# Three reorderings in a four-layer attention kernel: late next queries, an early first norm, a copy between maxima

## The chip, the cores and the metric

The kernel runs as one launch on one core of a Trainium2 chip. The metric is the device time of that launch in microseconds (us), as the median of several runs; lower is better. One further execution was recorded by the hardware profiler. Engines are PE (TensorE, the matrix unit), DVE (VectorE), ACT (ScalarE), POOL (GpSimd) and SP (SyncE, which here only starts transfers).

## What is computed

Four layers over a float32 input of 4 batches x 512 positions x 256 features, with a context of 4 x 64 x 192:

```
x = L0(x, ctx)   # cross attention (16 heads of 16), norm, feed-forward, residual
x = L1(x, ctx)   # norm, self attention (16 heads of 64); norm, cross attention; norm, gated feed-forward
x = L2(x, ctx)   # four state-space blocks over ctx followed by x
x = L3(x, ctx)   # norm, self attention (16 heads of 16); norm, cross attention; norm, feed-forward
```

The norms and one attention, cut to what matters here:

```
h = (x - mean(x)) * rsqrt(var(x) + eps) * g + b          # over the 256 features
p = exp(s - max(s)) / sum(exp(s - max(s)))               # s = q k^T, one row per query
out = p @ v ;  x = x + out @ Wo + bo
```

## The kernel before

Everything is float32 and feature-major: 128 features lie on the partitions, the 512 positions of a batch in the free dimension, so a linear layer is a row of 128x512 matmuls into one bank of PSUM each. The kernel is three blocks with a barrier between them: the first phase (layers one and two, that is L0 and L1, buffers `a_`), the middle one (the state-space layer, `m_`), which the change leaves alone, and the last phase (L3, buffers `c_`). There is no scheduler: each engine's program is written out by hand, in the order in which it runs, and every engine works strictly through its own list. A step waits with `wait_ge` for the semaphore count of the step it needs. A kernel is built twice, so that counts of steps written later are known. What sets the order around the change is therefore the source itself, separately for `pe`, `act` and `dve`.

In layers one, two and four the batches overlap in turns. A turn `(b, a)` holds the second half of batch `b` and the first half of batch `a = b + 1`; in layer one, small products for batch `n = a + 1` (its queries `query0`, lines 991 to 993, its context keys and values `context`, `keys2`, `values2`) lie between them. `x_of(b)` are two buffers: batch `n`'s rows can only be fetched after batch `b`'s were stored, once `l0 down 1 out` is done on DVE (the SP program, lines 914 to 920). `query0(n)` on PE waits for that fetch; its two results are copied by DVE (line 1259).

`Dense` holds the helpers. A norm is `pe_mean` (line 350), `dve_centre` (384), `act_squares` (368), `pe_var` (360), `act_rstd` (374 and 377), `dve_scale` (392 and 397). `pe_linear` (334) runs one product per output tile, `dve_residual` (405) adds it to x. These share a ring of two PSUM banks, `lin`: each `take` hands out the other bank, together with the step that empties its last contents, for which PE waits:

```
k = self.slots[self.i % len(self.slots)]
self.i += 1
freed, self.prog.emptied[k] = self.prog.emptied.get(k), (steps.sem, steps.at(emptied))
```

In layer two, a turn starts when the self attention of batch `b` ends: its output product `o1` (two tiles of 16 matmuls in the trace, each empties through `dve_residual`), then the first norm of `a` (`n1`) and the second of `b` (`n2`), interleaved step by step; then the queries `q1` of `a` and `q2` of `b`, eight tiles each.

In the last phase `pe_quads`, `act_quads`, `dve_quads` and `pool_self` (lines 663 to 795) run self attention in 16 steps of four units; a unit is one head and 128 queries, its scores fill one bank. In step `i` PE makes the four scores (678, ring `five` of five banks), then the transposes of units 4i-4 to 4i-1 (687, four each, ring `trn` of two banks), and in every second step a product with the values (702). DVE takes the four maxima (722), reciprocals of the sums (730) and copies the transposes of units 4i-3 and 4i-1 out of PSUM (737); ACT does the exponentials (783) and the copies of 4i-4 and 4i-2 (769); POOL divides (794). Unit 4i-1's transposes go into the bank that 4i-3's had, so they wait for DVE's copy of 4i-3.

## Time and profile before

| | us |
|---|---|
| median of 3 runs | 4527.23 (4520.4, 4527.23, 4527.54) |
| the profiled execution, its own time | 4522.28 |
| its span (first to last record) | 4520.2 |
| first phase, to the barrier | about 1440 |
| middle phase | about 2220 |
| last phase | about 850 |

The page gives PE 3775.1 us of busy time (84% of the span), DVE 3056.4, ACT 2351.8 and POOL 2115.0. The share of an engine is an average over three phases of different kind: in the first and the last PE is busy in most slices and the others are not, in the middle one DVE is busy throughout. So the trace has to be read stage by stage, by what PE waits for in each. The three runs lie 7 us apart.

### The profile page before, as it was taken

How to read it: one execution, taken by the hardware profiler on the slowest of the kernel's cores; microseconds unless marked ns; L12 is line 12 of the kernel's file. 1: busy time of each engine (PE TensorE's matmuls, PEld its weight loads, DVE VectorE, ACT ScalarE, POOL GpSimd, SP SyncE). 2: the span in 40 equal slices, each digit the busy share in tenths (PEclk: the TensorE clock that was granted, in tenths of full speed). 3: DMA queues.
4: the chain of work that ended last, by engine and by line, in shares of the span. 5: the costliest groups of instructions: out<-in, count | busy, mean ns of one | idle time of the engine just before them, and what ended most of it. 6: DMA issues, size and time to landing. Idle time of an engine off the chain costs nothing. (4 is left out here: it accounts for less than half of the span.)

```text
span 4520.2 us, 51563 instructions
## 1 busy us (share of the span) xinstructions
PE 3775.1 (84%) x16536; PEld 1949.7 (43%) x16536; DVE 3056.4 (68%) x4176; ACT 2351.8 (52%) x4473; POOL 2115.0 (47%) x2144
## 2 busy tenths in 40 slices
PE   8889999999986688877888788887888767878777
PEld 4434444444442244444444444444444434434343
DVE  4335435373451499998999989999899956464553
ACT  3234323242331477776777667776777634445352
POOL 1002112030120477877787777787777833222130
PEclk9999999999998799999999999999999989899999
DMA  3010000000001433222332233333332110000000
GB/s 144 28 49 17 1 19 1 10 10 10 5 1 44 103 92 85 73 84 78 89 85 80 74 96 88 85 93 84 94 85 73 49 60 1 11 1 12 1 6 5
DMA packets 135962, 228.48 MB, mean 51 GB/s; under 512 B 19280, under 2 KB 118864, under 8 KB 126864
## 3 DMA queue, kind: packets, MB, share of 16 engines
q1 hardware_dynamic: 135696, 225.20, 16.9%
q8 instruction: 135, 2.21, 0.2%
q14 instruction: 131, 1.07, 0.1%
HBM read 192.55 MB, written 32.60 MB: 50 GB/s over the span
## 5 line engine op out<-in xcount | busy, mean ns | idle before, releaser
L2039 POOL TENSOR_TENSOR m_db<-m_u,m_bb 128x512 f32<-128x512 f32 (+1 forms) x1280 | 1465.0, 1163 | 458.3 <-DVE m_hh L1991 455.4
L1991 DVE TENSOR_TENSOR_SCAN m_hh<-psum,m_kept,m_db 128x512 f32<-128x512 f32 (+1 forms) x1024 | 1195.9, 1202 | 29.9 <-POOL m_u L2084 17.5
L1790 ACT ACTIVATE psum<-m_dt,m_am 128x512 f32<-128x512 f32 (+1 forms) x1280 | 818.2, 644 | 407.0 <-DVE m_hh L1991 403.4
L1718 PE MATMUL psum<-cst,m_hh 128*128 128x128 f32 x4608 | 666.7, 286 | 323.5 <-DVE m_yt L2005 207.5
L1718 PEld LDWEIGHTS psum<-cst,m_hh 128*128 128x128 f32 x4608 | 525.6, 145 | 761.8 <-DVE m_yt L2005 424.0
L1728 PE MATMUL psum<-m_ys,cst 128*128 128x512 f32 x1024 | 553.0, 623 | 0.0
L2005 DVE SCALAR_TENSOR_TENSOR m_yt<-psum,m_bc,m_yt 128x512 f32<-128x512 f32 x600 | 437.6, 729 | 54.7 <-PE psum L1718 53.7
L794 POOL TENSOR_SCALAR a_pr<-a_pr,a_ri 128x512 f32<-128x512 f32 x256 | 173.8, 692 | 602.9 <-DVE a_ri L611 602.9
L794 POOL TENSOR_SCALAR c_pr<-c_pr,c_ri 128x512 f32<-128x512 f32 x256 | 173.7, 692 | 406.7 <-DVE c_ri L730 402.4
L1802 ACT ACTIVATE m_ys<-psum,m_bc 128x512 f32<-128x512 f32 x512 | 343.9, 672 | 24.1 <-PE psum L1718 22.7
L651 ACT ACTIVATE a_pr<-psum,a_mx 128x512 f32<-128x512 f32 x256 | 173.4, 682 | 264.4 <-DVE a_mx L601 264.4
L1604 PE MATMUL psum<-m_xn,m_wa 128*128 128x512 f32 (+1 forms) x640 | 295.3, 588 | 3.9 <-DVE m_xn L1949 3.6
L1991 DVE TENSOR_TENSOR_SCAN m_hh<-psum,m_db 128x384 f32<-128x384 f32 x256 | 232.3, 941 | 20.1 <-ACT m_kept L1811 11.7
L601 DVE TENSOR_REDUCE a_mx<-psum 128x2 f32<-128x1024 f32 x128 | 155.7, 1219 | 127.0 <-PE psum L551 127.0
L687 PE MATMUL psum<-cst,c_pr 128*128 128x128 f32 x1024 | 166.6, 303 | 81.0 <-DVE c_ptr L737 68.0
L722 DVE TENSOR_REDUCE c_mx<-psum 128x1 f32<-128x512 f32 x256 | 158.9, 683 | 81.6 <-PE psum L678 81.6
L1728 PEld LDWEIGHTS psum<-m_ys,cst 128*128 128x128 f32 x1024 | 170.7, 197 | 93.2 <-issue 67.7
L783 ACT ACTIVATE c_pr<-psum,c_mx 128x512 f32<-128x512 f32 x256 | 172.0, 691 | 46.9 <-DVE c_mx L722 46.9
L687 PEld LDWEIGHTS psum<-cst,c_pr 128*128 128x128 f32 x1024 | 120.8, 152 | 165.9 <-DVE c_ptr L737 82.7
L634 DVE COPY a_slots<-psum 128x512 f32<-128x512 f32 x256 | 162.3, 675 | 6.8 <-PE psum L561 6.8
L531 POOL TENSOR_TENSOR a_pr<-a_pr,a_ri 128x512 f32<-128x512 f32 x32 | 33.3, 1042 | 285.4 <-DVE a_ri L497 285.4
L561 PE MATMUL psum<-cst,a_pr 128*128 128x128 f32 x1024 | 151.3, 281 | 17.9 <-POOL a_pr L794 15.3
(242 smaller groups left out, 5621.7 us busy)
## 6 DMA issues: line engine op xcount, KB each, us to landing
m_bb<-b_rows SPq DMA_DIRECT2D x48, 1024.0 KB, 4.7
m_xr<-x_line SPq DMA_DIRECT2D x128, 192.0 KB, 3.9
m_bb<-b_rows SPq DMA_DIRECT2D x32, 768.0 KB, 4.5
m_xr<-x_line SPq DMA_DIRECT2D x128, 160.0 KB, 3.3
m_xr<-x_line SPq DMA_DIRECT2D x128, 128.0 KB, 3.1
m_xr<-x_line SPq DMA_DIRECT2D x128, 96.0 KB, 3.4
x_line<-m_xc SPq DMA_DIRECT2D x32, 192.0 KB, 4.5
m_wa<-w_in SPq DMA_DIRECT2D x4, 1376.0 KB, 7.5
```

Of the source, the lines that this page charges most:

```text
L651: nc.scalar.activation(self.pr[:, u % 6, :], self.full(f"{name} s {u}"), ACT.Exp, bias=self.nm[:, u % 8:u % 8 + 1], accum_out=self.smh[:, ...
L687: mm = nc.tensor.transpose(b[:, kt * P:(kt + 1) * P], self.pr[:, u % 6, kt * P:(kt + 1) * P], ident)
L783: nc.scalar.activation(self.pr[:, u % 6, :], self.full(f"{name} s {u}"), ACT.Exp, bias=self.nm[:, u % 8:u % 8 + 1], accum_out=self.smh[:, ...
L794: nc.gpsimd.tensor_scalar(self.pr[:, u % 6, :], self.pr[:, u % 6, :], self.rih[:, u % 8:u % 8 + 1], 1.0, ALU.mult, ALU.mult)\
L1604: mm = nc.tensor.matmul(full(job)[0:m, 0:w], lhs, rhs, start=k == 0, stop=k == n - 1)
L1718: mm = nc.tensor.transpose(s[:, e * P:(e + 1) * P], hh[:, n % 2, e, t * P:(t + 1) * P], ident)
L1728: nc.tensor.matmul(bank(SUMS[k]), ident, ys[:, k, :], start=n == 0, stop=n == LAST)\
L1790: nc.scalar.activation(bank(DECAY[u % len(DECAY)])[:, 0:w], dt[:, g % 2, e, 0:w], ACT.Exp, scale=am[:, layer_of(g) % 2, e * DS + n:e * DS ...
L1802: nc.scalar.activation(ys[:, k, :], bank(TURN_P), ACT.Identity, scale=bc[:, g % 2, t, DR + DS + n:DR + DS + n + 1], bias=0.0)\
L1991: nc.vector.tensor_tensor_scan(hh[:, n % 2, e, 0:w], bank(DECAY[u % len(DECAY)])[:, 0:w], db[:, u % 4, 0:w], kept[:, n, e:e + 1] if g % NI ...
L2005: nc.vector.scalar_tensor_tensor(y, bank(TURN_D), c, y, ALU.mult, ALU.add)\
L2039: nc.gpsimd.tensor_tensor(db[:, u % 4, 0:w], us[:, g % 2, e, 0:w], bb[:, at % 2, n % 4, 0:w], ALU.mult).then_inc(pool_done, pr.pool.step(f ...
```

## The change

Three lists are reordered; no operation is added or taken away, and no buffer is new.

Layer one: `query0(n)` goes from the middle of a turn (ahead of the products of attention weights with values) to its end, and the two `values2` products go one place forward each. On DVE the two copies of the queries follow `dve_scale` of `n0`.

Layer two: in a turn with both `b` and `a`, the mean of `n1` goes ahead of the output product `o1`, its variance between the two tiles of `o1`, and on DVE the whole norm goes ahead of both residual additions. The query tiles of `a` are spread around the steps of `n2`: tile 0, mean, tiles 1 and 2, variance, tiles 3 to 7.

Last phase: in each step DVE copies the transposes of unit 4i-3 after the second of the four maxima, no longer after the fourth.

```diff
@@ dve_quads
                     if i < plan.n:
-                        for u in range(4 * i, 4 * i + 4):
-                            maximum(u)
+                        maximum(4 * i)
+                        maximum(4 * i + 1)
                     if 1 <= i <= plan.n:
                         empty(4 * i - 3)
+                    if i < plan.n:
+                        maximum(4 * i + 2)
+                        maximum(4 * i + 3)
                     if i < plan.n:
                         inverse(2 * i)
@@ pe, layer one
-                        if n is not None:
-                            query0(n)
...
                         if n is not None:
                             keys2(n)
+                            values2(n, 0)
                         if a is not None:
                             st.pe_mean(pe, f"{a} n0", a0(a), (act_done, pr.act.at(f"{a} o0 1 out")))
                         if n is not None:
-                            values2(n, 0)
+                            values2(n, 1)
                         if a is not None:
                             st.pe_var(pe, f"{a} n0", norm0(a))
                         if n is not None:
-                            values2(n, 1)
+                            query0(n)
@@ pe, layer two
                         if b is not None:
+                            if a is not None:
+                                st.pe_mean(pe, f"{a} n1", x_of(a), (x_here[a % 2], x_count(1, a)))
                             pe.wait_ge(dve_done, pr.dve.at(f"{b} s1 o 7 out"))
-                            st.pe_linear(pe, f"{b} o1", mat(w1a, W1A["o"], 8, D), q1, 8, range(2), pr.dve)
-                        if a:
-                            st.pe_mean(pe, f"{a} n1", x_of(a), (x_here[a % 2], x_count(1, a)))
+                            st.pe_linear(pe, f"{b} o1", mat(w1a, W1A["o"], 8, D), q1, 8, [0], pr.dve)
+                            if a is not None:
+                                st.pe_var(pe, f"{a} n1", early)
+                            st.pe_linear(pe, f"{b} o1", mat(w1a, W1A["o"], 8, D), q1, 8, [1], pr.dve)
...
+                        queries([0])
                         if b is not None:
                             st.pe_mean(pe, f"{b} n2", x_of(b), (dve_done, pr.dve.at(f"{b} o1 1 out")))
-                        if a:
-                            st.pe_var(pe, f"{a} n1", early)
+                        queries([1, 2])
                         if b is not None:
                             st.pe_var(pe, f"{b} n2", late)
-                        if a is not None:
-                            pe.wait_ge(w1a_loaded, 16)
-                            pe.wait_ge(dve_done, pr.dve.at(f"{a} n1 out"))
-                            st.pe_linear(pe, f"{a} q1", mat(w1a, W1A["q"], 2, INNER), st.ln, 2, range(8), pr.act)
+                        queries([3, 4, 5, 6, 7])
@@ dve, layer one
-                        if n is not None:
-                            query0(n)
...
                             st.dve_scale(dve, f"{a} n0", norm0(a), vec("g"), vec("b"))
+                        if n is not None:
+                            query0(n)
@@ dve, layer two
+                        if a is not None and b is not None:
+                            st.dve_centre(dve, f"{a} n1", early, x_of(a))
+                            st.dve_scale(dve, f"{a} n1", early, vec("g1"), vec("n1"))
                         if b is not None:
                             st.dve_residual(dve, f"{b} o1", x_of(b), vec("o1"))
-                        if a:
-                            st.dve_centre(dve, f"{a} n1", early, x_of(a))
-                        if b is not None:
                             st.dve_centre(dve, f"{b} n2", late, x_of(b))
-                        if a:
-                            st.dve_scale(dve, f"{a} n1", early, vec("g1"), vec("n1"))
-                        if b is not None:
                             st.dve_scale(dve, f"{b} n2", late, vec("g2"), vec("n2"))
```

The program of ACT follows suit: squares and reciprocal root of `n1` first, then the query copies around the steps of `n2`.

PE in layer two, where a turn begins, is the first of three places. `L350` is a mean, `L360` a variance; `L334 ... a_w1a` with `a_slots` is `o1`, with `a_ln` the queries. Before:

```order
L334 MATMUL psum<-a_slots,a_w1a 128x512 [waits dve_done]
L334 MATMUL psum<-a_slots,a_w1a 128x512 x7
L334 MATMUL psum<-a_slots,a_w1a 128x512 [waits dve_done]
L334 MATMUL psum<-a_slots,a_w1a 128x512 x7
L350 MATMUL psum<-a_x,cst 128x512 [waits dve_done,xa_odd]
L350 MATMUL psum<-a_x,cst 128x512
L350 MATMUL psum<-a_x,cst 128x512 [waits dve_done]
L350 MATMUL psum<-a_x,cst 128x512
L360 MATMUL psum<-a_norm,cst 128x512 [waits act_done,dve_done]
L360 MATMUL psum<-a_norm,cst 128x512 [waits act_done]
L360 MATMUL psum<-a_slots,cst 128x512 [waits act_done,dve_done]
L360 MATMUL psum<-a_slots,cst 128x512 [waits act_done]
```

Now:

```order
L350 MATMUL psum<-a_x,cst 128x512 [waits dve_done,xa_odd]
L350 MATMUL psum<-a_x,cst 128x512
L334 MATMUL psum<-a_slots,a_w1a 128x512 [waits dve_done]
L334 MATMUL psum<-a_slots,a_w1a 128x512 x7
L360 MATMUL psum<-a_norm,cst 128x512 [waits act_done,dve_done]
L360 MATMUL psum<-a_norm,cst 128x512 [waits act_done]
L334 MATMUL psum<-a_slots,a_w1a 128x512 [waits dve_done]
L334 MATMUL psum<-a_slots,a_w1a 128x512 x7
L334 MATMUL psum<-a_ln,a_w1a 128x512 [waits act_done,dve_done,w1a_loaded]
L334 MATMUL psum<-a_ln,a_w1a 128x512
L350 MATMUL psum<-a_x,cst 128x512 [waits dve_done]
```

The mean went ahead of the first tile and the variance between the tiles; the second tile of `o1` still waits for DVE (`dve_done`), now with the bank of the first tile behind that wait.

DVE in the last phase, one step and the start of the next (`L722` maximum, `L737` copy, `L730` reciprocal). Before:

```order
L722 TENSOR_REDUCE c_mx<-psum 128x1 x4
L737 COPY c_ptr<-psum 128x4x128
L730 RECIPROCAL c_ri<-c_sm 128x2
L737 COPY c_ptr<-psum 128x4x128
L730 RECIPROCAL c_ri<-c_sm 128x2
L722 TENSOR_REDUCE c_mx<-psum 128x1 x4
```

Now, where the copy is at a later line of the file:

```order
L722 TENSOR_REDUCE c_mx<-psum 128x1 x2
L737 COPY c_ptr<-psum 128x4x128
L722 TENSOR_REDUCE c_mx<-psum 128x1 x2
L730 RECIPROCAL c_ri<-c_sm 128x2
L737 COPY c_ptr<-psum 128x4x128
L730 RECIPROCAL c_ri<-c_sm 128x2
L722 TENSOR_REDUCE c_mx<-psum 128x1 x2
```

One of the two copies went in front of the last two maxima; everything else kept its place.

PE in layer one, the end of a turn: `L945` with `a_slots,a_norm` is a `values2` product, `L334 ... a_x` the queries, `L334 ... a_ln` the first product of the next turn. Before:

```order
L350 MATMUL psum<-a_slots,cst 128x512 [waits act_done]
L350 MATMUL psum<-a_slots,cst 128x512
L945 MATMUL psum<-a_slots,a_norm 128x512 [waits act_done]
L945 MATMUL psum<-a_slots,a_norm 128x512
L360 MATMUL psum<-a_slots,cst 128x512 [waits act_done,dve_done]
L360 MATMUL psum<-a_slots,cst 128x512 [waits act_done]
L945 MATMUL psum<-a_slots,a_norm 128x512 [waits dve_done]
L945 MATMUL psum<-a_slots,a_norm 128x512
L334 MATMUL psum<-a_ln,a_region 128x512 [waits dve_done,w0b_loaded,act_done]
L334 MATMUL psum<-a_ln,a_region 128x512
```

Now (`L948` is the same line of the helper):

```order
L948 MATMUL psum<-a_slots,a_norm 128x512 [waits dve_done]
L948 MATMUL psum<-a_slots,a_norm 128x512
L360 MATMUL psum<-a_slots,cst 128x512 [waits act_done,dve_done]
L360 MATMUL psum<-a_slots,cst 128x512 [waits act_done]
L334 MATMUL psum<-a_x,a_region 128x512 [waits dve_done,xa_odd]
L334 MATMUL psum<-a_x,a_region 128x512
L334 MATMUL psum<-a_x,a_region 128x512 [waits act_done]
L334 MATMUL psum<-a_x,a_region 128x512
L334 MATMUL psum<-a_ln,a_region 128x512 [waits dve_done,w0b_loaded]
L334 MATMUL psum<-a_ln,a_region 128x512
```

The queries of the next batch took the last place in the turn and the variance comes after both `values2` products.

## Rows read from the trace of the kernel before

**Rows 1.** The page: busy time of each engine, and 40 slices of the span.
```profile
PE 3775.1 (84%) x16536; PEld 1949.7 (43%) x16536; DVE 3056.4 (68%) x4176; ACT 2351.8 (52%) x4473; POOL 2115.0 (47%) x2144
...
PE   8889999999986688877888788887888767878777
DVE  4335435373451499998999989999899956464553
```

**Rows 2.** Timeline of PE in layer one; columns: start, us, operation, idle before and releaser.
```profile
47.73 3.60 PE L334 MATMUL psum<-a_x,a_region 128*128 128x512 f32 x8
51.17 7.03 PE L945 MATMUL psum<-a_slots 128*128 128x512 f32 x16
...
70.77 1.94 PE L360 MATMUL psum<-a_slots,cst 128*128 128x512 f32 x4
72.55 1.88 PE L945 MATMUL psum<-a_slots,a_norm 128*128 128x512 f32 x4
76.66 1.96 PE L334 MATMUL psum<-a_ln,a_region 128*128 128x512 f32 x4 [2.23 <-DVE a_ln L397]
...
121.79 6.12 PE L334 MATMUL psum<-a_x,a_region 128*128 128x512 f32 x8 [6.86 <-DMA a_x<-x_in]
...
199.95 6.30 PE L334 MATMUL psum<-a_x,a_region 128*128 128x512 f32 x8 [6.74 <-DMA a_x<-x_in]
...
272.23 7.13 PE L945 MATMUL psum<-a_slots 128*128 128x512 f32 x16 [0.69 <-ACT a_slots L1190]
```

**Rows 3.** Timeline of DVE: the last step of the norm that ends a turn.
```profile
75.53 0.88 DVE L397 TENSOR_SCALAR a_ln<-a_ln,a_v 128x512 f32<-128x512 f32 x2
```

**Rows 4.** Timeline of PE where the first turn of layer two begins.
```profile
480.75 14.00 PE L334 MATMUL psum<-a_slots,a_w1a 128*128 128x512 f32 x32 [0.79 <-DVE a_slots L617]
...
499.79 1.88 PE L360 MATMUL psum<-a_slots,cst 128*128 128x512 f32 x4
503.82 13.97 PE L334 MATMUL psum<-a_ln,a_w1a 128*128 128x512 f32 x32 [2.15 <-issue]
```

**Rows 5.** Timeline of DVE there: a residual addition.
```profile
487.99 0.75 DVE L405 SCALAR_TENSOR_TENSOR a_x<-psum,a_v,a_x 128x512 f32<-128x512 f32 x1 [7.30 <-PE psum L334]
```

**Rows 6.** Stretches: us, then busy us of PE, PEld, DVE, ACT, POOL, granted clock, DMA.
```profile
115.00:135.00 20.00, 13.21 (x28) 5.98 (x29) 2.78 (x5) 0.56 (x1) 0.00 (x0) 0.83 0.15 53
502.00:520.00 18.00, 16.18 (x38) 7.33 (x39) 3.84 (x8) 6.26 (x11) 0.00 (x0) 1.00 0.00 1
774.50:779.00 4.50, 4.50 (x7) 1.96 (x8) 2.00 (x4) 0.60 (x1) 0.00 (x0) 0.62 0.00 0
3700.00:3800.00 100.00, 75.48 (x624) 43.15 (x628) 63.44 (x129) 63.32 (x165) 43.44 (x64) 0.91 0.00 1
```

**Rows 7.** Waits of PE, 3700 to 3800 us; columns: waits, releaser, us, times, longest.
```profile
PE psum L687 <- DVE c_ptr L737: 17.1, 15, 1.5
```

**Rows 8.** Timeline of PE in the last phase, steps without and with L702.
```profile
3758.37 1.14 PE L678 MATMUL psum<-c_k,c_q 32*128 32x512 f32 x8
...
3763.30 1.14 PE L678 MATMUL psum<-c_k,c_q 32*128 32x512 f32 x8
...
3776.89 1.14 PE L678 MATMUL psum<-c_k,c_q 32*128 32x512 f32 x8
...
3781.24 0.65 PE L687 MATMUL psum<-cst,c_pr 128*128 128x128 f32 x4 [1.28 <-DVE c_ptr L737]
3781.82 1.93 PE L702 MATMUL psum<-c_ptr,c_v3s 128*32 128x256 f32 x32
3783.69 1.14 PE L678 MATMUL psum<-c_k,c_q 32*128 32x512 f32 x8
```

**Rows 9.** Timeline of DVE, the step that begins at 3776.89.
```profile
3778.10 2.48 DVE L722 TENSOR_REDUCE c_mx<-psum 128x1 f32<-128x512 f32 x4 [0.34 <-PE psum L678]
3780.50 0.68 DVE L737 COPY c_ptr<-psum 128x512 f32<-128x512 f32 x1
```

**Rows 10.** Timeline of ACT: third exponential of the step that begins at 3758.37.
```profile
3761.96 0.69 ACT L783 ACTIVATE c_pr<-psum,c_mx 128x512 f32<-128x512 f32 x1
```

More of the change, by code:

```diff
@@ L1211, in _, with queries @@
                     for b, a in turns:
-                        if a:
+                        if a is not None and b is not None:
                             st.act_squares(act, f"{a} n1", early)
+                            st.act_rstd(act, f"{a} n1", early)
+                        def queries(tiles):
+                            if a is not None:
+                                for j in tiles:
+                                    copy(f"{a} q1 {j}", q1[:, j, :], st.full(f"{a} q1 {j}"), scale=0.125)
+                        queries([0])
                         if b is not None:
                             st.act_squares(act, f"{b} n2", late)
-                        if a:
-                            st.act_rstd(act, f"{a} n1", early)
+                        queries([1, 2])
                         if b is not None:
                             st.act_rstd(act, f"{b} n2", late)
-                        if a is not None:
-                            for j in range(8):
-                                copy(f"{a} q1 {j}", q1[:, j, :], st.full(f"{a} q1 {j}"), scale=0.125)
+                        queries([3, 4, 5, 6, 7])
                         def keys(u):
@@ L1349, in _ @@
                         if n is not None:
-                            values2(n, 0)
+                            values2(n, 1)
                         if a is not None:
                             st.dve_scale(dve, f"{a} n0", norm0(a), vec("g"), vec("b"))
+                        if n is not None:
+                            query0(n)
+                        if a is not None:
                             for j in range(2):
@@ L1357, in _ @@
                         if n is not None:
[L1358 removed]
                             keys2(n)
                     for b, a in turns:
+                        if a is not None and b is not None:
+                            st.dve_centre(dve, f"{a} n1", early, x_of(a))
+                            st.dve_scale(dve, f"{a} n1", early, vec("g1"), vec("n1"))
                         if b is not None:
                             st.dve_residual(dve, f"{b} o1", x_of(b), vec("o1"))
[L1364 to L1366 removed]
                             st.dve_centre(dve, f"{b} n2", late, x_of(b))
[L1368 to L1370 removed]
                             st.dve_scale(dve, f"{b} n2", late, vec("g2"), vec("n2"))
```

9 lines of the change are left out of this document (6 added, 3 removed).

## The prediction

> **What bounds the kernel now.** I read the page first, then, phase by phase, the timeline and the waits of PE, because PE is busy in eight or nine tenths of most slices while DVE is nearly full only in the middle phase [rows 1]. The change leaves the middle alone. In the first and the last phase, then, time is PE's work plus the stretches in which PE waits, and an edit is worth what it takes from or adds to those. The other engines count where PE's next step hangs on them.
>
> In layer one the reader should see two long gaps [rows 2]: the query product of the next batch (L334 with a_x) waits 6.86 and 6.74 us for its input to arrive from memory, and then takes 6.12 and 6.30 us, against 3.60 for the same eight matmuls at 47.73, where the rows were there already. Around the first gap the granted clock was 0.83 over 20 us [rows 6]; 0.17 below full, at half clock, is 6.8 us. The other gap of every turn is 2.23 us before the next turn's first product, waiting for the norm.
>
> Where a turn of layer two begins PE waits 0.79 us for the last copy of the attention output and 2.15 us ahead of the queries [rows 4]. Each of three such turns has both.
>
> In the last phase, step after step, PE waits for one copy by DVE: 17.1 us in 15 waits, in one batch of four [rows 7]. The four transposes at 3781.24 start 0.06 us after DVE's copy ends (3780.50 plus 0.68), and that copy starts right behind four maxima [rows 8, 9]. That is the largest stock of waiting in reach of this change.
>
> **Layer one.** The query product moves to the turn's end, some 23 us later (from 51.17 to behind the variance, 72.55, and a values product), so rows that came 6.9 us late are there. Taken away: 6.86 + 6.74 = 13.6 us, and the slow clock behind them, 6.12 + 6.30 - 2 x 3.60 = 5.2 us. SP's list is as it was: store, fetch, keep the context. What the product covered is bare now: the products of weights and values wait for ACT's last copy of the transposes, as they already do in the turn without a next batch, 0.69 us [rows 2]. At the turn's end the variance starts at 70.77, the norm's last step ends on DVE at 75.53 + 0.88 = 76.41 [rows 3], and the next turn starts at 76.66, 5.89 us after the variance. Before, that part and the queries (47.73 to 51.17, 3.44 us) make 9.33. Now one values product of four matmuls (half of 3.44, 1.72) comes ahead of the variance, and behind the norm DVE makes two query copies, each priced like an addition at 0.75 [rows 5], while PE's 3.44 us of queries lie under the norm. The next turn waits for the second copy: 5.64 + 1.50 + 0.06 = 7.2 us after the variance's start. 1.72 + 7.2 + 0.69 = 9.6, so 0.3 more in each of three turns, 0.9 in all. Queued behind the query copies on DVE are the residual additions and the mask of the context keys; their readers come in the next turn, far enough off, and cost nothing. If this cover went, a late first maximum of the next turn would show at once. Sum: -13.6 - 5.2 + 0.9 = -17.9.
>
> **Layer two.** The mean of the next batch now fills the 0.79 us wait, and spread query tiles fill the 2.15. But the ring `lin` has two banks, handed out strictly in turn. The takes now are: attention output 7, mean, o1 tile 0, variance, o1 tile 1. Tile 1 gets the bank of tile 0 and must wait for DVE's residual addition of tile 0, which on DVE now stands behind the whole norm, and the norm's scaling waits for ACT's root, and that for the variance that PE makes just before tile 1. So PE waits for a chain that it has only just started. Its length, from the same norm in layer one [rows 2, 3]: 5.64 us from the variance's start to its end, plus the addition 0.75 [rows 5] plus 0.06, 6.45; PE's own variance fills 1.78 of it (70.77 to the next product at 72.55). That leaves a new wait of about 4.7 us. Behind tile 1 nothing more is late: the mean of n2 waits for the addition of tile 1, under query tile 0. Per turn +4.7 - 0.79 - 2.15 = +1.7, for three turns +5.2.
>
> Then the clock. After the wait of 2.15 us at 503.82 it stayed full (1.00), after the same wait in the second turn it was 0.62 over 4.5 us [rows 6], 3.4 us at half clock, which loses 1.7 us of work; the 6.86 us wait lost 2.5. For 4.7 us I take 1.7 in every turn, less the one that is there: 3 x 1.7 - 1.7 = +3.4. Bounds: nothing (as at 503.82) and 2.5 each. Layer two: +8.6. The Trainium skill, TensorE: Matmul & The Clock Gate, in its table of goals, says that idle gaps between bursts of matmuls bring the array back to half clock, which speaks against this part of the change. The trace agrees at 121.79 and leaves it open at 2.15 us, and by that rule alone the sum keeps all three terms.
>
> **Last phase.** No duration changes; DVE's copy of unit 4i-3 moves ahead of two maxima. Four maxima occupy 3778.10 to 3780.50, so 0.60 us each from start to start [rows 9]. In a step that begins with scores at time 0: maxima from 1.21, the copy now from 2.41 instead of 3.61, PE's transposes from 3.15 instead of 4.35, ended at 3.73 (0.58, from 3781.24 to 3781.82 [rows 8]). In a step with the value product (L702, 1.87 us) the next scores come at 5.6 instead of 6.80 (3783.69 - 3776.89): -1.20. In a step without it another chain ends last. `five` gives the next scores the bank of unit 4i+2, whose exponential now waits for a maximum that is one copy later: maximum 3.01 to 3.69, exponential (0.69 [rows 10]) 3.75 to 4.44, scores at 4.50 instead of 4.93 (3763.30 - 3758.37 [rows 8]): -0.43. Before, that exponential ended at 3762.65, 0.65 ahead of the scores at 3763.30, so the copy's 0.60 just fits. A batch has seven steps of each kind, leaving out the first, which starts on an empty pipeline: 7 x 1.20 + 7 x 0.43 = 11.4, in four batches -45.6 us. Bounds: the whole wait, 4 x 17.1 = 68, and nothing in steps without L702, 4 x 8.4 = 33.6. Behind the delayed maxima are two exponentials, one reciprocal (it follows the fourth maximum, which ends where the copy used to, so POOL gets it at the same time) and POOL's divisions, hidden by the next scores.
>
> The Trainium skill, VectorE: DVE Perf Modes, section The DRAIN you can't avoid, says that the next operation does not start until the pipe has emptied, which would make each maximum cost its full 0.68 us; the rows show 0.60 from start to start. By the page the copy would move by 1.36 us, past the wait of 1.28, and the sum would be some 2 us better; I go by the rows.
>
> **The sum.** -17.9 + 8.6 - 45.6 = -54.9 us on the profiled execution of 4522.28 us (its span is 4520.2): 4467.4. The median of the runs is 4.95 us above that execution; I forecast 4468 and keep the difference in the range. A measurement of this kernel tells a change from none at about 0.2%, 9 us.
>
> **Rivals.**
> - Only the steps with L702 gain, because ACT's exponentials rule the others. For it: the margin of 0.65 us against 0.60 is thin. Against: in the rows nothing but that copy would delay it further. -33.6 in place of -45.6: 4480. 13%.
> - The clock recovers in the last phase. It was 0.91 over 100 us of self attention [rows 6], 18 us at half clock, at most 9 us lost per batch; with less waiting a third of that may come back, -12: 4456. 15%.
> - Layer two stays clear, if DVE gets to the addition in time after all: without +8.6, and with the two waits gone (-8.8) and their slow clock (-1.7): 4449. Only the ring speaks against it, but plainly. 5%.
> - The copy does not stand ready after two maxima, because POOL's division of unit 4i-3 or its transposes are late; it then holds DVE and both later maxima. Half the gain, -23: 4490. 5%.
> - The layer one edit doesn't do what it says: another wait for the same transfer takes its place. The rows were only 6.9 us late, against 23 us of grace. Without -17.9: 4485. 3%.
> - Slower: ACT bounds every step. Then a maximum delayed by 0.60 us delays each of 15 steps in 4 batches, +36, and the sum is -17.9 + 8.6 + 36: 4549. It decides if exponential 4i+2 ends where the next scores start; in the rows it ends 0.65 us before, without L702, so this needs the exponentials to lengthen as well. 3%.
>
> **How the numbers follow.** My forecast has the remaining 56% and by itself spans 4457 to 4479 (clock terms and runs). The range 4449 to 4484 takes in the first three rivals and leaves about 15% out. Faster by over 0.2%: all but the last rival and some unseen mishap, 0.95; within 0.2%: 0.02; slower: 0.03.
>
> **What would show it.** In the profile after: no wait for a DMA at L334 in layer one, the query product at 3.6 us; a wait of 4.7 us at L334 for DVE's addition (L405) in the middle of o1, three times, with a lower clock behind it; in the last phase DVE's waiting entry of 17.1 us shrunk to a few, steps of about 4.5 and 5.6 us, and self attention of a batch some 11 us shorter. I am wrong if steps with L702 stay above 6.3 us, if PE waits at L678 for ACT take the place of those at L687, or if o1 runs through without a gap.

## The result, and the profile after

| | before | after |
|---|---|---|
| median, us (4 runs each) | 4523.81 (4520.28 to 4527.54) | 4466.74 (4463.8 to 4470.18) |
| profiled execution, us | 4522.28 | 4463.8 |
| its span, us | 4520.2 | 4461.8 |
| granted clock, mean | 0.952 | 0.959 |

The ratio is 0.9874, with a 95% interval of 0.9857 to 0.9891: the change makes the kernel 57 us faster. The forecast was 4468, within 4449 to 4484.

The page of after, busy time and slices, to be held against [rows 1]:

```profile
PE 3750.1 (84%) x16536; PEld 1936.9 (43%) x16536; DVE 3055.0 (68%) x4176; ACT 2360.3 (53%) x4473; POOL 2116.0 (47%) x2144
...
PE   8999999999987578887888888887788868888787
```

The work is the same to the instruction. PE's busy time fell by 25 us all the same: a matmul at half clock is busy for longer, and the mean granted clock rose from 0.952 to 0.959. The other 33 us are idle time of PE that went.

Where the time went can be read by stages. Each row below is the distance from the start of one product of PE to the start of another, in the trace of before and in that of after, in us. A self attention runs from its first scores to its last value product (L578 in layer two, L702 in the last phase), the cross attention with the hidden layer from its queries to the last product of the hidden layer. The rows end at the last product, 18.6 us ahead of the end of the span in both.

| stage | before | after | difference | forecast |
|---|---|---|---|---|
| start to first query product | 19.44 | 21.91 | +2.5 | 0 |
| layer one, to the first queries of layer two | 310.42 | 290.63 | -19.8 | -17.9 |
| layer two, three starts of a turn (last value product to queries of the cross attention) | 39.62, 41.32, 39.62 | 42.50, 42.53, 42.56 | +7.0 | +8.6 |
| layer two, four self attentions | 106.02, 106.03, 106.04, 107.32 | 107.39, 107.41, 107.39, 107.40 | +4.2 | 0 |
| layer two, three times cross attention and hidden layer | 111.08, 111.07, 112.58 | 112.59, 112.56, 112.57 | +3.0 | 0 |
| rest of layer two | | | -0.1 | 0 |
| middle phase | 2239.19 | 2232.25 | -6.9 | 0 |
| last phase, four self attentions | 98.86, 97.15, 97.83, 97.19 | 85.56, 85.11, 84.87, 84.96 | -50.5 | -45.6 |
| rest of the last phase | 444.50 | 446.83 | +2.3 | 0 |
| sum | | | -58.3 | -54.9 |

**Layer one.** The timeline of PE in after, same columns as [rows 2], from the first turn and the end of the second:

```profile
50.99 8.83 PE L948 MATMUL psum<-a_slots 128*128 128x512 f32 x16 [0.69 <-ACT a_slots L1198]
...
74.10 1.93 PE L360 MATMUL psum<-a_slots,cst 128*128 128x512 f32 x4
...
120.09 7.13 PE L948 MATMUL psum<-a_slots 128*128 128x512 f32 x16 [0.69 <-ACT a_slots L1198]
...
143.28 3.60 PE L334 MATMUL psum<-a_x,a_region 128*128 128x512 f32 x8
148.51 1.98 PE L334 MATMUL psum<-a_late_ln,a_region 128*128 128x512 f32 x4 [1.64 <-DVE a_slots L1271]
```

The query product at 143.28 has no wait and takes 3.60 us, where [rows 2] had 6.86 us of wait and 6.12 of work. In its old place there are 0.69 us for ACT, and ahead of the next turn 1.64 us for DVE's second query copy in the place of 2.23 for the norm. In the first turn the sixteen matmuls in that old place take 8.83 us, in the second 7.13: the first turn has a slow stretch (granted clock 0.89 over 45 to 60 us) that it did not have before.

**Layer two.** PE at the start of the first turn, and of the third:

```profile
463.93 1.98 PE L350 MATMUL psum<-a_x,cst 128*128 128x512 f32 x4
465.75 7.03 PE L334 MATMUL psum<-a_slots,a_w1a 128*128 128x512 f32 x16
472.62 1.88 PE L360 MATMUL psum<-a_norm,cst 128*128 128x512 f32 x4
479.04 8.52 PE L334 MATMUL psum<-a_slots,a_w1a 128*128 128x512 f32 x16 [4.53 <-DVE a_x L405]
487.39 1.88 PE L334 MATMUL psum<-a_ln,a_w1a 128*128 128x512 f32 x4
...
1031.88 8.58 PE L334 MATMUL psum<-a_slots,a_w1a 128*128 128x512 f32 x16 [4.54 <-DVE a_x L405]
```

Both waits of [rows 4] are gone, and a new one of 4.5 us stands between the two tiles of `o1`. What it waits for is in the rows of the two other engines, ACT first:

```profile
474.54 0.69 ACT L374 ACTIVATE a_rs<-psum,a_eps 128x512 f32<-128x512 f32 x1 [6.63 <-PE psum L360]
475.26 0.63 ACT L377 ACTIVATE a_rs<-a_rs 128x512 f32<-128x512 f32 x1
```

and DVE:

```profile
475.99 1.41 DVE L392 SCALAR_TENSOR_TENSOR a_ln<-a_norm,a_v,a_rs 128x512 f32<-128x512 f32 x2 [8.75 <-ACT a_rs L377]
477.32 0.88 DVE L397 TENSOR_SCALAR a_ln<-a_ln,a_v 128x512 f32<-128x512 f32 x2
478.23 0.75 DVE L405 SCALAR_TENSOR_TENSOR a_x<-psum,a_v,a_x 128x512 f32<-128x512 f32 x1
```

Tile 0 of `o1` is complete by the time the variance starts at 472.62. Its eviction (L405) comes at 478.23, behind a root and a scaling that could not begin before that variance, and PE starts tile 1 at 479.04, 0.06 us after it (478.23 plus 0.75). Tile 1's sixteen matmuls then take 8.52 us, against 7.03 for tile 0.

**The clock.** Stretches of after, columns as in [rows 6]:

```profile
120.00:140.00 20.00, 19.86 (x77) 11.60 (x78) 5.07 (x14) 2.53 (x6) 0.00 (x0) 1.00 0.15 53
359.00:363.00 4.00, 4.00 (x16) 1.87 (x12) 2.42 (x4) 2.06 (x7) 2.25 (x4) 0.58 0.00 0
478.00:483.00 5.00, 3.96 (x6) 1.80 (x7) 0.94 (x2) 0.00 (x0) 0.00 (x0) 0.66 0.00 0
3690.00:3775.50 85.50, 70.62 (x608) 40.47 (x608) 63.28 (x129) 63.86 (x163) 43.22 (x64) 0.96 0.01 1
```

Layer one is at full clock in the second turn, where it was at 0.83. Behind the new wait it is 0.66 over 5 us, 3.4 us of them at half clock. And at 359, at the head of the first self attention, where no line was touched, it is 0.58 over 4 us. Before, the stretch that answers to it (376 to 380) had 1.00, as the first of these two stretches of before shows; the second is the last phase, about the first batch's self attention:

```profile
376.00:380.00 4.00, 3.93 (x20) 1.88 (x20) 2.89 (x6) 2.66 (x8) 2.71 (x4) 1.00 0.01 4
...
3690.00:3775.50 85.50, 64.62 (x486) 36.94 (x484) 54.65 (x113) 49.49 (x134) 32.57 (x48) 0.92 0.01 2
```

**Last phase.** The waits of PE in after from 3690 to 3790 us, as in [rows 7]:

```profile
PE psum L678 <- ACT c_pr L786: 9.3, 9, 3.0
PE psum L687 <- ACT c_ptr L772: 3.8, 15, 0.3
```

DVE's entry of 17.1 us is gone. In its place PE waits at L678 (scores) for ACT: 9 times, 0.84 us in the usual case, once 3.0. The one of 3.0 us comes at the second step of a batch, and before has it too (3.04), so 6.3 us of this waiting are new. PE's timeline, a step with L702 and one without (as [rows 8]):

```profile
3715.45 1.14 PE L678 MATMUL psum<-c_k,c_q 32*128 32x512 f32 x8 [0.84 <-ACT c_pr L786]
...
3719.17 1.93 PE L702 MATMUL psum<-c_ptr,c_v3s 128*32 128x256 f32 x32
3721.04 1.14 PE L678 MATMUL psum<-c_k,c_q 32*128 32x512 f32 x8
...
3725.69 1.14 PE L678 MATMUL psum<-c_k,c_q 32*128 32x512 f32 x8 [0.84 <-ACT c_pr L786]
```

The steps are 5.59 us with L702 (before 6.80) and 4.65 without (before 4.93). In after nearly every step has these lengths. In before two to four steps of each batch were stretched, as the one with this row, in which the 32 small matmuls take 3.43 us and not 1.93 and the step 8.51:

```profile
3768.45 3.43 PE L702 MATMUL psum<-c_ptr,c_v3s 128*32 128x256 f32 x32
```

Over the four batches such stretching beyond the second step comes to some 10 us in before and to nothing in after.

DVE and ACT in the step without L702 that begins at 3721.04; DVE:

```profile
3722.25 1.29 DVE L722 TENSOR_REDUCE c_mx<-psum 128x1 f32<-128x512 f32 x2 [1.43 <-PE psum L678]
3723.45 0.68 DVE L737 COPY c_ptr<-psum 128x512 f32<-128x512 f32 x1
3724.05 1.28 DVE L722 TENSOR_REDUCE c_mx<-psum 128x1 f32<-128x512 f32 x2
```

ACT:

```profile
3724.76 0.69 ACT L786 ACTIVATE c_pr<-psum,c_mx 128x512 f32<-128x512 f32 x1
3725.35 0.19 ACT L786 ACTIVATION_READ_ACCUMULATOR c_pr<-psum,c_mx 128x1 f32 x1
```

The copy starts 2.41 us into the step and the third maximum 3.01, both to the hundredth where the forecast had them. The third exponential starts at 3.72. But the scores do not go when it ends: the instruction that reads out its sum follows, until 3725.54, and the scores come 0.15 us behind that, at 4.65.

### The profile page after: what moved, and what is told of

Its sections match the earlier page's. It is cut to its first block and busy times, and to the rows that moved or that the text cites. A ratio compares the mean times of both kernels' runs of the same rounds, so it can differ in the third digit from the quotient of the medians.

```text
span 4461.8 us, 51571 instructions
## 1 busy us (share of the span) xinstructions
PE 3750.1 (84%) x16536; PEld 1936.9 (43%) x16536; DVE 3055.0 (68%) x4176; ACT 2360.3 (53%) x4473; POOL 2116.0 (47%) x2144
## 3 DMA queue, kind: packets, MB, share of 16 engines
q1 hardware_dynamic: 135696, 225.20, 17.1%
## 5 line engine op out<-in xcount | busy, mean ns | idle before, releaser
L2001 DVE TENSOR_TENSOR_SCAN m_hh<-psum,m_db 128x384 f32<-128x384 f32 x256 | 232.0, 939 | 20.1 <-ACT m_kept L1821 11.7
L722 DVE TENSOR_REDUCE c_mx<-psum 128x1 f32<-128x512 f32 x256 | 163.7, 682 | 59.0 <-PE psum L678 59.0
L561 PEld LDWEIGHTS psum<-cst,a_pr 128*128 128x128 f32 x1024 | 111.3, 143 | 129.1 <-DVE a_slots L634 64.5
```

Of the source, the lines that this page charges most:

```text
L561: mm = nc.tensor.transpose(b[:, kt * P:(kt + 1) * P], self.pr[:, u % 6, kt * P:(kt + 1) * P], ident)
L722: nc.vector.tensor_reduce(self.nm[:, u % 8:u % 8 + 1], self.full(f"{name} s {u}"), AX.X, ALU.max, negate=True).then_inc(dve_done, p.dve.st ...
L2001: nc.vector.tensor_tensor_scan(hh[:, n % 2, e, 0:w], bank(DECAY[u % len(DECAY)])[:, 0:w], db[:, u % 4, 0:w], kept[:, n, e:e + 1] if g % NI ...
```

## The experiments

Two theories for the whole. The first is that of the forecast: three separate terms (two gains, one loss) that add up, with the loss made by the order of DVE's list around the ring of two banks. The rival: the parts are tied together by the clock, so that what one of them brings depends on the others, and the waits are only where the loss shows. The first three runs do one part each on the kernel before; the fourth mends what the first theory calls the fault. These four ran on one chip, where before had a median of 4520.3 us (15 runs).

**The last phase alone.** The kernel before with the edit in `dve_quads` only:

```diff
-                        for u in range(4 * i, 4 * i + 4):
-                            maximum(u)
+                        maximum(4 * i)
+                        maximum(4 * i + 1)
                     if 1 <= i <= plan.n:
                         empty(4 * i - 3)
+                    if i < plan.n:
+                        maximum(4 * i + 2)
+                        maximum(4 * i + 3)
```

> The kernel before with the reordering of the last phase alone. Theory A (the parts add up, and the last phase carries the gain): 46 to 51 us less than before, about 4475; in the self attention of each batch steps with L702 about 5.6 us instead of 6.8, steps without it about 4.6 instead of 4.93, PE's waits for the moved copy nearly gone. Rival (the gain in the last phase is luck of the clock, since granted clock rose there as well): under 30 us, with steps still at 6.8. The first phase stays as it was, with 13.6 us of waiting for the transfer of x.

Measured: 4473.65 us, ratio 0.9894 (0.988 to 0.9907), 46.7 less than before. The four self attentions take 85.57, 85.20, 84.99 and 85.10 us, 50.2 less in all, the same as in after. The term of the last phase stands by itself; it needs neither of the other parts.

**Layer one alone.** The kernel before with the two lists of layer one as in the change:

```diff
@@ pe, layer one
-                        if n is not None:
-                            query0(n)
...
+                        if n is not None:
+                            query0(n)
```

> The kernel before with the late queries of layer one alone. Theory A: 18 to 20 us less than before, about 4505: no wait for the transfer of x, query products at 3.6 us, per turn a new wait of 0.69 us and about 1.6 us at the turn's end. Rival (the wait only moves): less than 9 us less, with a wait of some us for the transfer at the new place or a slow clock elsewhere in layer one.

Measured: 4504.99 us, ratio 0.9965 (0.9951 to 0.9978), 15.3 less, with 10 to 22 in the interval. By its trace layer one takes 290.34 us, 20.1 less than before, and the start of the kernel 1.4 more (20.83 against 19.44). So the stage gained what the theory says and a little more in that one execution. The median gained less than the 18 to 20 us expected, which its interval takes in, and more than the rival's 9; no wait for the transfer is left in its trace.

**Layer two alone.** The kernel before with the lists of layer two as in the change (mean and variance around `o1`, the norm ahead of the residual additions on DVE):

```diff
@@ dve, layer two
+                        if a is not None and b is not None:
+                            st.dve_centre(dve, f"{a} n1", early, x_of(a))
+                            st.dve_scale(dve, f"{a} n1", early, vec("g1"), vec("n1"))
                         if b is not None:
                             st.dve_residual(dve, f"{b} o1", x_of(b), vec("o1"))
...
```

> The kernel before with the reordering of layer two alone. Theory A (tile 1 of o1 waits for the bank of tile 0): slower by 5 us of waits, and by up to 14 with the slow clock behind them, so 4529 to 4538; a wait of 4.5 us for L405 in three turns. Rival (the slow clock in layer two came from another alignment and not from these waits): slower by 5 us or less. If the spread query tiles were a gain as they stand, it would be faster by 9 us; neither theory expects that.

Measured: 4531.98 us, ratio 1.0025 (1.0016 to 1.0034): 11.7 more. This part of the change makes the kernel slower. The three starts of a turn take 44.08, 44.09 and 44.10 us, 11.7 more than before; the rest of layer two takes 2.5 more in this execution (self attentions +4.0, cross attention with hidden layer -1.5). PE's timeline:

```profile
498.37 10.09 PE L334 MATMUL psum<-a_slots,a_w1a 128*128 128x512 f32 x16 [4.54 <-DVE a_x L405]
```

The wait is the same 4.54 us as in after, and what differs is the clock behind it (0.70 over the 10 us from 498.4, in after 0.83 over the 8.5 us from 479): tile 1 takes 10.09 us here, 8.52 in after, 7.03 at full clock. The price of the wait is thus 1.5 us of slow clock in one kernel and 3.1 in the other, with the same instructions around it.

**The eviction ahead of the scaling.** After, with DVE's residual addition of tile 0 of `o1` between the centring of `n1` and its scaling, so that bank and norm no longer hang together; nothing else moves (`dve_residual` gets an argument that names the tiles, left out here):

```diff
                             st.dve_centre(dve, f"{a} n1", early, x_of(a))
+                        if b is not None:
+                            st.dve_residual(dve, f"{b} o1", x_of(b), vec("o1"), [0])
+                        if a is not None and b is not None:
                             st.dve_scale(dve, f"{a} n1", early, vec("g1"), vec("n1"))
                         if b is not None:
-                            st.dve_residual(dve, f"{b} o1", x_of(b), vec("o1"))
+                            st.dve_residual(dve, f"{b} o1", x_of(b), vec("o1"), [1])
```

> The changed kernel, with one edit: on DVE the residual addition of o1 tile 0 goes ahead of the norm's scaling, so that the bank is free when tile 1 wants it. Theory A: the wait of 4.5 us in three turns goes, 13.6 us, and the lowered clock right behind it in each turn (3.4 us at half, 1.7 us of work each) with it: 14 to 19 us less than the changed kernel, 4448 to 4453. Rival (something else holds tile 1, or the wait comes back at the queries, which need the norm): less than 5 us less than the changed kernel, with a new wait before the first query tile.

Measured: 4439.88 us (4434.13 to 4445.58), ratio 0.9821 (0.9806 to 0.9835). That beats both kernels. Its timeline of PE, the same place:

```profile
463.24 7.03 PE L334 MATMUL psum<-a_slots,a_w1a 128*128 128x512 f32 x16
470.10 1.88 PE L360 MATMUL psum<-a_norm,cst 128*128 128x512 f32 x4
471.82 7.03 PE L334 MATMUL psum<-a_slots,a_w1a 128*128 128x512 f32 x16
478.69 1.88 PE L334 MATMUL psum<-a_ln,a_w1a 128*128 128x512 f32 x4
```

its DVE:

```profile
470.37 0.75 DVE L405 SCALAR_TENSOR_TENSOR a_x<-psum,a_v,a_x 128x512 f32<-128x512 f32 x1 [5.65 <-PE psum L334]
```

and the clock there:

```profile
462.00:500.00 38.00, 38.00 (x90) 16.85 (x89) 8.71 (x15) 10.86 (x18) 0.00 (x0) 1.00 0.00 0
```

One addition in another place, and PE is busy in all of 38 us. The starts of a turn take 36.31, 36.31 and 36.32 us, 18.6 less than in after, and the two profiled spans differ by the same amount (4461.8 and 4443.1). Against before (39.62, 41.32, 39.62) they gain 11.6, so the idea of this part of the change was good and only the addition stood wrong. By the medians, each against its own runs of before, the gain over after is 80.4 - 57.1 = 23.3 us. The four executions lie at 4434 (two) and 4445 (two), and the profiled one is of the latter, while that of after is the fastest of its four, so 18.7 is on the low side. 14 to 19 were expected: the wait and the clock behind it give that much, and what is above it is of the size of the scatter. No new wait came ahead of the first query tile, as the rival had it.

The next four ran together, where before had a median of 4519.1 us (7 runs).

**The copy after three maxima.** After, with the copy one maximum later:

```diff
+                    k = 3
                     if i < plan.n:
-                        maximum(4 * i)
-                        maximum(4 * i + 1)
+                        for u in range(4 * i, 4 * i + k):
+                            maximum(u)
                     if 1 <= i <= plan.n:
                         empty(4 * i - 3)
                     if i < plan.n:
-                        maximum(4 * i + 2)
-                        maximum(4 * i + 3)
+                        for u in range(4 * i + k, 4 * i + 4):
+                            maximum(u)
```

> The changed kernel, with the copy of unit 4i-3 after the third maximum instead of the second. Theory A (a step with L702 ends with the copy and the transposes behind it, a step without it with the third exponential, so the copy's place trades the one for the other): the copy comes 0.60 us later, steps with L702 go from 5.59 to about 6.2; the third maximum is no longer behind it, so steps without L702 go from 4.65 to about 4.45. Per batch 7 x 0.6 - 7 x 0.2 = 2.8 us more, 11 us in all: 4478. Rival (only the copy matters): both kinds 0.6 longer, 34 us more: 4500. Rival (any place ahead of the last maximum is as good): no change.

Measured: 4475.02 us, ratio 0.9898 (0.9883 to 0.9913). The steps are 6.19 us with L702 and 4.51 without, as in these rows of PE:

```profile
3717.87 1.14 PE L678 MATMUL psum<-c_k,c_q 32*128 32x512 f32 x8
...
3721.61 0.66 PE L687 MATMUL psum<-cst,c_pr 128*128 128x128 f32 x4 [0.61 <-DVE c_ptr L737]
...
3724.06 1.14 PE L678 MATMUL psum<-c_k,c_q 32*128 32x512 f32 x8
...
3728.57 1.14 PE L678 MATMUL psum<-c_k,c_q 32*128 32x512 f32 x8
```

With the maximum back ahead of the copy, the scores no longer wait for ACT in the steps without L702, and those gain 0.14 us; the steps with L702 lose 0.60, the distance from one maximum to the next. Steps of 6.2 and 4.45 were expected, and the median is 3 us under the 4478. Neither rival fits: not both kinds of step are longer, and the place is not indifferent. Both chains are where the theory has them, and each has its own best place for the copy.

**The copy after one maximum.** The same edit of after with one maximum ahead of the copy and three behind it:

```diff
+                    k = 1
...
```

> The changed kernel, with the copy of unit 4i-3 after the first maximum. Theory A: the copy is not ready then, it must wait for its transposes (2.16 us after the scores begin, against 1.81 when the first maximum is done), so it gains only 0.2 us, and the second to fourth maxima and exponentials come later by 0.4 to 1 us: steps without L702 go from 4.65 to about 5.1, steps with L702 from 5.59 to about 5.5; about 2.5 us more per batch, 10 in all: 4477. Rival (the earlier the copy, the better): 4 x 14 x 0.6 = 34 us less than the changed kernel, 4433.

Measured: 4486.99 us, ratio 0.9926 (0.9911 to 0.9941), 10 us more than expected. PE:

```profile
3714.82 1.14 PE L678 MATMUL psum<-c_k,c_q 32*128 32x512 f32 x8
...
3719.94 1.14 PE L678 MATMUL psum<-c_k,c_q 32*128 32x512 f32 x8 [1.51 <-ACT c_pr L787]
...
3725.33 1.14 PE L678 MATMUL psum<-c_k,c_q 32*128 32x512 f32 x8
```

DVE:

```profile
3716.03 0.69 DVE L722 TENSOR_REDUCE c_mx<-psum 128x1 f32<-128x512 f32 x1 [0.77 <-PE psum L678]
3717.02 0.69 DVE L737 COPY c_ptr<-psum 128x512 f32<-128x512 f32 x1 [0.30 <-PE psum L687]
3717.63 1.88 DVE L722 TENSOR_REDUCE c_mx<-psum 128x1 f32<-128x512 f32 x3
```

Here the copy comes too early. DVE stands 0.30 us before the transposes are there, and now all three later maxima are late: the wait for ACT grows from 0.84 to 1.51 us. The steps, 5.12 and 5.40, are as expected (5.1 and 5.5). The total is not. From the steps the four self attentions should take 7 x (5.12 - 4.65) + 7 x (5.40 - 5.59) = +2.0 each against after, 8 in all; they take 90.24, 88.22, 91.81 and 88.83, 18.6 in all. Of the other 11 us, 6.2 are four stretched steps of the first and the third batch (6.81 and 7.03 in the place of 5.40, 6.75 in that of 5.12, and the last one), where the granted clock was 0.94 over each batch. Some 2.6 are not clock: the end of a batch, from its last scores to its last value product, is 9.49 at full clock against 9.02 in after, with a new wait for ACT's copy,

```profile
3780.10 1.09 PE L687 MATMUL psum<-cst,c_pr 128*128 128x128 f32 x8 [0.71 <-ACT c_ptr L773]
```

and the sum counted a saving of 0.19 there. The last 2 lie in the second step of a batch. So the expectation was short by the clock and by the end of the batch.

**The layer-two fault mended, and the copy placed by kind of step.** The kernel of the fourth run, with the copy after two maxima where the step has L702 and after three where it has not:

```diff
+                    k = 2 if i % 2 and i > 1 else 3
                     if i < plan.n:
-                        maximum(4 * i)
-                        maximum(4 * i + 1)
+                        for u in range(4 * i, 4 * i + k):
+                            maximum(u)
...
```

> e4 (residual addition ahead of the norm's scaling) with, in the last phase, the copy after the second maximum in steps with L702 and after the third in steps without it. Theory A: steps with L702 stay at 5.6, those without go from 4.65 to about 4.45: 7 x 0.2 x 4 = 6 us less than e4, 4434, at the edge of what can be told. Rival (the two kinds of step are coupled, what one gains the next gives back): as e4, 4440.

Measured: 4442.5 us, ratio 0.9829 (0.9814 to 0.9844): no gain over the fourth run (4439.88). The steps are as they should be, 5.59 and 4.51, so the two kinds of step are not coupled as the rival had it, and the four self attentions take 83.85, 84.30, 84.32 and 83.55, 5.0 us less in all than in the fourth run. The stages ahead of and between them are longer by 6.5 (37.39, 110.23, 108.99 and 108.28, against 35.12, 107.93, 105.66 and 109.64), with the same instructions. Their clock is lower, as the stretch from the first self attention to the second shows, in the fourth run:

```profile
3765.00:3875.00 110.00, 87.82 (x245) 40.64 (x243) 49.19 (x89) 33.58 (x66) 11.11 (x13) 0.92 0.03 11
```

and in this one:

```profile
3765.00:3875.00 110.00, 88.77 (x237) 40.62 (x235) 47.38 (x85) 31.41 (x60) 11.01 (x12) 0.89 0.03 11
```

0.03 of the full clock over 110 us is 6.6 us more at half clock, or some 3.3 us of work. The saving in the steps is real, and this execution did not keep it. Of the 6.5 us, 2.3 lie ahead of the first saved step, so the saving cannot have caused them. The other 4.3 lie between the batches. These three stages come to 323.2 to 323.6 us in the four kernels that have the copy after two maxima in every step, to 325.6 (copy after three), 328.8 (after one) and 327.5 (by kind of step) in the others, and to 322.7 to 325.1 in the three kernels that have it after four. So the place of the copy may have a price there too, which no expectation had; that it does is not shown.

**Without the layer-two part.** After, with layer two as before, so the sum of the first two runs:

```diff
@@ dve, layer two
-                        if a is not None and b is not None:
-                            st.dve_centre(dve, f"{a} n1", early, x_of(a))
-                            st.dve_scale(dve, f"{a} n1", early, vec("g1"), vec("n1"))
...
```

> The changed kernel without its reordering of layer two (layer one and the last phase alone). Theory A: 12 us less than the changed kernel, 4455, as layer two alone cost 12; and 15 more than e4, in which that reordering has lost its wait. Rival (the slow clocks of layer two are a matter of where the turns fall, so the parts do not add up): the same as the changed kernel within 5 us.

Measured: 4453.63 us (4451.95 to 4456.54), ratio 0.9855 (0.9838 to 0.9871). That is 13 less than the median of the change as it was made (8 less, each against its own runs of before, which is within what these medians can tell), where 12 was expected. By the traces layer two takes 11.3 less than in after, 5.3 of it in the starts of turns and 6.0 in the self attentions and the stages of cross attention and hidden layer. With the addition put right it is the other way round, and that kernel is 13.7 below this one (15 against the own runs of before, as expected). The starts of a turn are back at 39.62, 41.32 and 41.32 us. The single parts add up to -46.7 - 15.3 + 11.7 = -50.3, the change as a whole measured -57; the two agree within what the medians allow (each is uncertain by some 4 to 8 us). So the parts add up as far as medians can tell. In the small, though, the traces bear the rival out: the same starts of turns take 44.1 us where layer two is edited alone and 42.5 with all three parts, 4.7 us in all, while fewer of the other stages are long. How one part sets the clock of another is not shown.

## Why the prediction was right

It had -54.9 us, and so 4467.4 us for the profiled execution, which took 4463.8; the stages sum to -58.3. The difference of 3.4 is made of errors of both signs, some 27 us of them by stages, so that the total came this near is in part luck. The mechanisms of the three terms are borne out by the runs; the clock is what the sum had least right.

**Layer one, -17.9 forecast, -19.8 found.** The waits for DMA and the slow queries went as worked out, [rows 2]. The term missed that two more stretches of slow clock, at the ends of turns, would go with them, 1.7 us each: the granted clock was 0.72 over 152 to 158 us before and is 1.00 over 150 to 157 now. It missed as well that the first turn would get one, 8.83 us for 7.13 at 50.99. The small debts came as forecast, 0.69 us for ACT and 1.6 for the second query copy: -13.6 - 5.2 - 3.5 + 1.7 + 0.8 = -19.8.

**Layer two, starts of a turn, +8.6 forecast, +7.0 found.** From the variance's start to tile 1's the forecast had 6.45 us, and it is 6.42 (472.62 to 479.04), of which 1.72 would pass without a wait, as in the fourth run (470.10 to 471.82). So the new wait costs 4.70 a turn by the starts, though the idle time before tile 1 is 4.53: groups of matmuls that follow one another overlap by some 0.16 us in the timeline, and a wait loses that too. For the same reason the two removed waits, 0.79 and 2.15, were worth 3.3 and not 2.94 (39.62 against 36.31 in the fourth run). That makes 3 x (4.70 - 3.31) = +4.2 for the 5.2. The clock took 1.5 us a turn instead of 1.7, 3 x 1.5 - 1.7 = +2.8 for 3.4. The run with the addition ahead of the scaling shows the mechanism: it takes away the order on DVE and nothing of the work, and wait and slow clock are both gone. The Trainium skill, TensorE: Matmul & The Clock Gate, in its table of goals, has idle gaps bring back half clock; behind 4.5 us of wait the trace agrees in all three turns (0.66 over 478 to 483), and the clock stays at 1.00 where no gap is left.

**The rest of layer two, 0 forecast, +7.1 found.** This is the step that failed here: "three turns" was where I let the slow clock act. The self attentions have two lengths, 106.0 and 107.4 us, and the cross attention with the hidden layer two as well, 111.1 and 112.6. Before, two of these seven stages were long; in after all seven were. The difference is a stretch at half clock, as at 359. Such stretches do not need the edit, but they are more frequent with it. In the four kernels with layer two untouched, two, two, three and three of the seven stages are long; in the six that have its new order it is four (edited alone), four and five (addition mended), and all seven in after and in the two others that have its wait and both other parts. So the forecast left out about half of what this part of the change costs: of the 11.3 us between the kernel without the layer-two part and after, 6.0 are in stages where no line was touched. Why the order at the start of a turn sets the clock further on is not shown. Which stages are long differs even where the instructions do not: before and the kernel with the last phase alone have the same instructions up to the barrier, and only the number of long stages, two, is the same in them.

**Last phase, -45.6 forecast, -50.5 found.** The steps with L702 gained 1.21, against 1.20. Those without gained 0.28 and not 0.43: the working had the scores start 0.06 us behind the third exponential, at 4.50, and they start 0.15 behind the read of its sum, at 4.65. With 7 x (1.21 + 0.28) = 10.4 a batch, 41.7 in all, the steps account for four fifths. The other 9 us are the clock: the stretched steps of before, some 10 us, are gone, and the second steps are a little longer. Over the four batches the granted clock was 0.91, 0.91, 0.95 and 0.93 before and is 0.96, 0.98, 0.98 and 0.98 after. The rival that gave it -12 was right in kind and nearly in size, and was counted out of the sum at 15%. So of the two errors, +4 and -9, one took away half of the other. One of the three signs that the forecast had named for being wrong did come: PE waits at L678 for ACT, 0.84 us in each of seven steps of a batch. These are the steps without L702, in which the forecast itself had the third exponential end last, so the sign was worded too widely and does not speak against the chain; it tells where the missing 0.15 us are. The rule of the Trainium skill, VectorE: DVE Perf Modes, section The DRAIN you can't avoid, was rightly passed over: the maxima of after are again 0.60 us from start to start at 0.68 each (3722.25 to 3723.45 for two), and the copy moved by two of these, 1.20 us, not by 1.36. The same paragraph of that section says further on that an operation that is not held starts earlier, which the forecast left out and with which these rows agree.

**What no term had.** The middle phase, which no edit touches, took 6.9 us less. In the ten traces of this study it takes between 2228.8 and 2239.2 us, and that of before is the longest of them. So 58.4 us of difference between two executions contain some 7 that belong to no term; whether they are chance or follow from the edits is not shown, as each kernel has one trace. Start and rest of the last phase, +4.8, offset most of it. The stages that the edits touch sum to -63.3, forecast -54.9.

## What to carry to other kernels

When an order of work is changed, go through the rings of buffers as well as the engines: list who takes each bank in the new order, and see that the operation that frees it does not stand behind a chain that the waiting engine itself has only just started. One addition moved ahead of that chain was worth more (18.7 us by the spans) than the layer-two part had lost. And where a copy can stand at several points in a run of equal operations, find for each kind of step the two chains on either side of it: the best place is the first at which the copy's input is ready, unless the operations pushed back are themselves waited for.

## What the runs showed of the hardware that was not expected

- A wait of the same length cost different clock: 4.54 us ahead of the same sixteen matmuls was followed by 8.52 us of them in one kernel and 10.09 in another, against 7.03 at full clock.
- Waits of some 2 us that both kernels have are followed by a slow stretch in some places and not in others, at 1.3 to 1.7 us each, and edits elsewhere move these. The head of the self attention at 359 is one. It happens with the same instructions too: before and the kernel with the last phase alone do not differ up to the barrier, and the second self attention takes 106.0 us in one and 107.4 in the other. The Trainium skill, TensorE: Matmul & The Clock Gate, Part 1, tells of the start of a kernel that the count of slow matmuls differs from run to run; here such stretches differ in the midst of a kernel too.
- A saving of 5 us in four stages (copy placed by kind of step) stood beside 6.5 us more in the stages ahead of and between them, at a lower clock and with the instructions unchanged. That the saving caused it is not shown.
- An exponential with a sum is two instructions on ACT, 0.69 and 0.19 us, and PE started 0.15 us after the end of the second, 0.24 after that of the exponential, in each of the steps of the first batch of after that waited 0.84 us for it.
